# Gated projections of a four-layer triangle-multiplication kernel: low half of the weights in 64-row matmuls, pairs of units, wide units without mask

## The reference, cut to what matters

```python
xn = layer_norm(_gn(x), norm_a, norm_b)
left = (xn @ Wl + bl) * sigmoid(xn @ Wlg + blg)
right = (xn @ Wr + br) * sigmoid(xn @ Wrg + brg)
out_gate = sigmoid(xn @ Wog + bog)
out = einsum('bkjd,bkid->bijd', left, right) / n
out = layer_norm(out, on_a, on_b) * out_gate
x = x + (out @ Wo + bo)
```

## Time and profile before

| | us |
|---|---|
| median of 3 runs | 2210.91 (2204.99 to 2215.15) |
| the profiled execution | 2208.5 |
| its span in the profile | 2206.5 |
| eight `project` stages, from first matmul to last product | 562.3 |

### The profile page before, as it was taken

The page is one execution under the profiler, slowest core; times in us unless marked ns, Lnnn a source line. Parts: engine busy times, 40 slices in busy tenths (PEclk is TensorE's granted clock), DMA queues, the critical chain, the costliest instruction groups (busy, mean ns, idle before and its releaser), DMA issues. The chain is left out here.

```text
span 2206.5 us, 46371 instructions
## 1 busy us (share of the span) xinstructions
PE 1972.7 (89%) x13956; PEld 1401.8 (64%) x13956; DVE 1735.3 (79%) x2934; ACT 1691.9 (77%) x2730; POOL 624.5 (28%) x590
## 2 busy tenths in 40 slices
PE   5798979699898998989989899899998989899998
PEld 4433959455433988965633598886553369798665
DVE  6788899989588977878958897877766888687665
ACT  3588869789888857759978785776997877596676
POOL 0100828265200000026410280742871000000655
PEclk8899999999999999999999999999999999999999
DMA  9488938279788928259969973917997984663798
GB/s 396 163 263 285 280 88 229 82 286 381 243 267 264 319 77 294 88 216 398 414 211 283 272 195 120 286 52 263 407 389 226 278 293 158 222 203 124 282 357 305
DMA packets 429367, 549.52 MB, mean 249 GB/s; under 512 B 14640, under 2 KB 325936, under 8 KB 412848
## 3 DMA queue, kind: packets, MB, share of 16 engines
q1 hardware_dynamic: 427648, 538.38, 72.6%
q10 hardware_dynamic: 1584, 9.51, 1.1%
HBM read 371.67 MB, written 176.16 MB: 248 GB/s over the span
## 5 line engine op out<-in xcount | busy, mean ns | idle before, releaser
L798 PE MATMUL bank<-whigh,kept 128*128 128x128 f16 x4096 | 507.7, 228 | 62.2 <-DMA kept<-XH 21.7
L798 PEld LDWEIGHTS bank<-whigh,kept 128*128 128x128 f16 x4096 | 466.5, 125 | 69.7 <-issue 56.2
L798 PE MATMUL bank<-wlow,kept 128*128 128x128 f16 x4096 | 506.7, 227 | 0.0
L798 PEld LDWEIGHTS bank<-wlow,kept 128*128 128x128 f16 x4096 | 467.1, 125 | 0.0
L1556 POOL TENSOR_TENSOR LR<-LR 128x512 f32<-128x512 f32 x128 | 186.6, 1477 | 526.9 <-DVE LR L1602 507.4
L820 ACT ACTIVATE sigs<-bank,small 128x256 f32<-128x256 f32 x512 | 236.7, 475 | 64.4 <-PE bank L798 58.0
L1547 POOL TENSOR_TENSOR LR<-LR,sum 128x2048 f32<-128x2048 f32 x30 | 136.6, 4553 | 510.7 <-DVE LR L1365 510.7
L662 PE MATMUL bank<-LR,cen 128*128 128x512 f32 x512 | 254.6, 623 | 20.9 <-DMA LR<-XT 8.6
L820 ACT ACTIVATE squares<-bank,small 128x256 f32<-128x256 f32 x512 | 236.1, 475 | 13.3 <-PE bank L798 5.6
L669 PE MATMUL bank<-LR,kst 128*128 128x512 f32 x512 | 240.9, 593 | 5.2 <-ACT LR L690 5.2
L835 POOL TENSOR_TENSOR msgs<-sigs,mask_sb 128x256 f32<-128x256 f32 x192 | 125.9, 670 | 381.8 <-ACT sigs L820 375.3
(11 more groups left out here) (174 smaller groups left out, 3745.3 us busy)
## 6 DMA issues: line engine op xcount, KB each, us to landing
kept<-XH SPq DMA_DIRECT2D x128, 512.0 KB, 5.5
LR<-XT SPq DMA_DIRECT2D x64, 1024.0 KB, 9.4
kept<-XHA SPq DMA_DIRECT2D x128, 512.0 KB, 4.6
LR<-XT SPq DMA_DIRECT2D x112, 512.0 KB, 5.5
XT<-LR SPq DMA_DIRECT2D x56, 1024.0 KB, 8.4
LR<-XH SPq DMA_DIRECT2D x64, 512.0 KB, 6.6
LR<-XHA SPq DMA_DIRECT2D x64, 512.0 KB, 5.8
OS<-kept SPq DMA_DIRECT2D x12, 2048.0 KB, 7.6
```

The lines of the kernel that those rows point to most:

```text
L798: last = pe.matmul(bank(g)[:, j * P:(j + 1) * P], tokens, w[:, half * P:(half + 1) * P], start=part == 0, stop=part == 1)
```

## The change

- Rows: in DRAM and in the chunk buffers the channels' rows are no longer interleaved high, low, high, low, but in two blocks of 64 partitions: for side 0 high then low, for side 1 low then high (`XH` and `XHA` have four blocks in front). The rows of the projected weights follow (`K_DROP`, `K_LAST`); the output gate's 64 columns keep the old order, so `project_pe` makes six matmuls instead of three, DVE one more small operation in `fold`, and the constants have 256 more columns.
- `wlow` is multiplied only by the high rows: 64-row matmuls, on partitions 0 to 63 for side 0 and 64 to 127 for side 1, in turn. The product low x wlow is dropped.
- Order on PE: a unit q is two banks, one for each side (`bank(2q)`, `bank(2q+1)`). PE does the eight 128-row matmuls of one unit, the eight of the next, then the sixteen 64-row ones of both. It waits before a unit's 128-row matmuls until the products of the unit four before it are done.
- Layers without mask: ACT and DVE take a whole unit, 128x512, in one instruction. Masked layers keep 128x256 groups.
- `store_xh` of the layers without mask issues four DMAs of 64 partitions for a chunk instead of two of 128 (`per` is 64 for all).

```diff
@@ -115,8 +115,8 @@
             return s
 
         XT = nc.dram_tensor("XT", [NT, 8, P, COLS], F32).ap()
-        XH = nc.dram_tensor("XH", [NT, C, 2, 2, 8, 8, 256], F16).ap()
-        XHA = nc.dram_tensor("XHA", [C, 2, 2, NT, N // 2, P], F16).ap()
+        XH = nc.dram_tensor("XH", [NT, 4, C, 8, 8, 256], F16).ap()
+        XHA = nc.dram_tensor("XHA", [4, C, NT, N // 2, P], F16).ap()
         OS = nc.dram_tensor("OS", [NT, N // 16, P, 2, 256], F32).ap()
 
 
@@ -260,20 +260,21 @@
         def xh_rows(n, s, k_is_b):
 
             if k_is_b:
-                return XH[bass.ds(n // 8, 1), :, :, s, :, bass.ds(n % 8, 1), :] \
-                    .rearrange("o c w v g f -> (o c w) v (g f)")
-            return XHA[:, :, s, :, bass.ds(8 * n, 8), :].rearrange("c w t j a -> (c w) t (j a)")
+                return XH[bass.ds(n // 8, 1), 2 * s:2 * s + 2, :, :, bass.ds(n % 8, 1), :] \
+                    .rearrange("o w c v g f -> (o w c) v (g f)")
+            return XHA[2 * s:2 * s + 2, :, :, bass.ds(8 * n, 8), :].rearrange("w c t j a -> (w c) t (j a)")
 
         def store_xh(sp, n, part, buf, k_is_b, stored_):
 
             if k_is_b:
                 for s in range(2):
-                    sp.dma_start(XH[bass.ds(n // 8, 1), :, part, s, :, bass.ds(n % 8, 1), :]
+                    sp.dma_start(XH[bass.ds(n // 8, 1), 2 * s + (part ^ s), :, :, bass.ds(n % 8, 1), :]
                                  .rearrange("o c v g f -> (o c) v (g f)"), xh_cols(buf[s::2, :], k_is_b)) \
                         .then_inc(stored_.s, 16)
             else:
-                sp.dma_start(XHA[:, part, :, :, bass.ds(8 * n, 8), :].rearrange("c s t j a -> c s t (j a)"),
-                             xh_cols(buf, k_is_b)).then_inc(stored_.s, 16)
+                for s in range(2):
+                    sp.dma_start(XHA[2 * s + (part ^ s), :, :, bass.ds(8 * n, 8), :].rearrange("c t j a -> c t (j a)"),
+                                 xh_cols(buf[s::2, :], k_is_b)).then_inc(stored_.s, 16)
 
         def xh_cols(buf, k_is_b):
 
@@ -320,18 +321,21 @@
...
             def project_pe(pe):
-                pe.wait_ge(folded.s, folded.n + (3 if late else 2))
-                pe.matmul(projected_w, K(K_DROP, C), wfold, start=True, stop=False)
-                pe.matmul(projected_w, blast, w_cat, start=False, stop=False)
-                pe.matmul(projected_w, K(K_LAST, 1), prm[0:1, W_BIAS:W_BIAS + 320],
-                          start=False, stop=True).then_inc(weights.s, 1)
+                pe.wait_ge(folded.s, folded.n + (4 if late else 3))
+                for cols, drop, blast_, end in ((slice(0, 256), K_DROP, blast, K_LAST),
+                                                (slice(256, 320), K_DROP_GATE, blast_gate, K_LAST_GATE)):
+                    pe.matmul(projected_w[:, cols], K(drop, C), wfold[:, cols], start=True, stop=False)
+                    pe.matmul(projected_w[:, cols], blast_, w_cat[:, cols], start=False, stop=False)
+                    last = pe.matmul(projected_w[:, cols], K(end, 1), prm[0:1, W_BIAS:W_BIAS + 320][:, cols],
+                                     start=False, stop=True)
+                last.then_inc(weights.s, 1)
                 if late:
                     pe.matmul(centered_w, K(K_CENTER_OUT), wout_w, start=True, stop=True)
                     pe.matmul(biased_w, w_out, vec(V_OB), start=True, stop=True).then_inc(late_folded.s, 1)
...
@@ -747,14 +752,19 @@
             k_is_b, masked = layer["k_is_b"], layer["masked"]
             whigh, wlow = halves_of_w[number % 2]
             dest = LRb if layer["low"] else LR
-            gate, unscale = msg if masked else sig, unscales[number % 2]
+            unscale = unscales[number % 2]
             by_vector, by_pool = (1, 5), (0, 2, 3, 4, 6, 7)
+            each = 2 if masked else 1
+            wide_gate = [v[:, u * BANK:(u + 1) * BANK].rearrange("p (c s m) -> p c s m", s=2, m=4)
+                         for v in rings[0] for u in range(2)]
 
             def where(n, g):
 
-                if k_is_b:
-                    return g // 4, 16 * n + 4 * (g % 4)
-                return g // 2 % 2, P * (g // 4) + 8 * n + 4 * (g % 2)
+                q, s = divmod(g, 2)
+                return s, 16 * n + 4 * q
+
+            def both_sides(q):
+                return banks[q][:, :].rearrange("p (s m c) -> p c s m", s=2, m=4)
 
             @block.sync
             def _(sp):
...
-                        sp.wait_ge(projected.s, projected.n + 8 * n - 24)
+                        sp.wait_ge(projected.s, projected.n + 4 * each * n - 12 * each)
...
+                sides_last = [(s, j) for j in range(4) for s in range(2)]
+
+                def tokens(h, s, q, j, rows):
+                    x = xh_b[h][s]
+                    if k_is_b:
+                        return x.rearrange("p (b r) -> p b r", r=16)[rows, :, 4 * q + j]
+                    return x[rows, (4 * q + j) * P:(4 * q + j + 1) * P]
+
                 with pe.Fori(0, NCH // 4) as i:
                     for h in range(4):
                         pe.wait_ge(landed[h].s, landed[h].n + 32 * i + 32)
-                        for g in range(8):
-                            pe.wait_ge(products_ready.s, products_ready.n + 32 * i + 8 * h + g - 7)
-                            for j in range(4):
-                                x = xh_b[h][g // 4]
-                                if k_is_b:
-                                    tokens = x.rearrange("p (b r) -> p b r", r=16)[:, :, 4 * (g % 4) + j]
-                                else:
-                                    tokens = x[:, (4 * (g % 4) + j) * P:(4 * (g % 4) + j + 1) * P]
-                                for part, w in enumerate((whigh, wlow)):
-                                    last = pe.matmul(bank(g)[:, j * P:(j + 1) * P], tokens,
-                                                     w[:, half * P:(half + 1) * P], start=part == 0, stop=part == 1)
-                            last.then_inc(projected.s, 1)
+                        for two in range(2):
+                            for q in (2 * two, 2 * two + 1):
+                                unit = 16 * i + 4 * h + q
+                                pe.wait_ge(products_ready.s, products_ready.n + each * unit - 3 * each)
+                                for s, j in sides_last:
+                                    pe.matmul(bank(2 * q + s)[:, j * P:(j + 1) * P], tokens(h, s, q, j, slice(0, P)),
+                                              whigh[:, half * P:(half + 1) * P], start=j == 0, stop=False)
+                            for q in (2 * two, 2 * two + 1):
+                                for s, j in sides_last:
+                                    rows = slice(C * s, C * s + C)
+                                    last = pe.matmul(bank(2 * q + s)[:, j * P:(j + 1) * P], tokens(h, s, q, j, rows),
+                                                     wlow[rows, half * P:(half + 1) * P], start=False, stop=j == 3)
+                                    if j == 3 and (masked or s == 1):
...
+                else:
+                    with act.Fori(0, NCH // 4) as i:
+                        for h in range(4):
+                            for q in range(4):
+                                unit = 16 * i + 4 * h + q
+                                act.wait_ge(projected.s, projected.n + unit + 1)
+                                if half == 1 and q >= 2:
+                                    act.wait_ge(summed.s, summed.n)
+                                act.wait_ge(products_ready.s, products_ready.n + unit - 3)
+                                act.activation(wide_gate[q], both_sides(q)[:, C:, :, :],
+                                               ACT.Sigmoid, scale=unscale).then_inc(gates_ready.s, 1)
...
+                else:
+                    with dve.Fori(0, NCH // 4) as i:
+                        for h in range(4):
+                            for q in range(4):
+                                unit = 16 * i + 4 * h + q
+                                m = 8 * (4 * i + h) + 4 * (q % 2)
+                                dve.wait_ge(gates_ready.s, gates_ready.n + unit + 1)
+                                dve.scalar_tensor_tensor(dest[:, q // 2, :, :].rearrange("p c (s r) -> p c s r", s=2)
+                                                         [:, :, :, bass.ds(m, 4)],
+                                                         both_sides(q)[:, 0:C, :, :], unscale, wide_gate[q],
+                                                         ALU.mult, ALU.mult).then_inc(products_ready.s, 1)
...
@@ -925,11 +965,12 @@
             ut, vb = at(c)
             for part in range(2):
                 buf = homes.xh[c % len(homes.xh)][part]
+                blocks = slice(0, 4, 3) if part == 0 else slice(1, 3)
                 if layer["k_is_b"]:
-                    sp.dma_start(buf, XH[ut, :, part, :, vb, :, :].rearrange("c s g f -> c s (g f)")) \
```

(7 more changed lines are left out.)

97 lines of the change are left out of this document (48 added, 49 removed).

## The result

The changed kernel takes **2245.15 us**, the median of 4 runs (2239.93 to 2246.47); the kernel before, in 4 runs beside it, 2207.95 (2203.84 to 2215.15). The ratio is 1.0161, with a 95% interval of 1.0144 to 1.0177: 1.6% slower. The profiled execution has a span of 2242.7 us, against 2206.5 before, so 36.2 us are to be found.

What follows compares the result with a forecast made beforehand. PE sets the pace before; after the change, the way round of a pair of units through ACT, POOL and DVE. Masked stages 28, unmasked 3, stores 3, fold and constants 2: +36 on 2208.5, forecast 2244 us, range 2196 to 2297.

Steps and rivals of the forecast that it cites:

- The way round with mask, 4.56 us a chunk: Masked `project` stages: PE to ACT, POOL, DVE and back for a pair of units takes 4.56 us a chunk, against 4.01.
- The masked stages, +28: Four masked `project` stages: thirteen slower chunks each, a longer end, -0.5 in the first three chunks; +28 us in all.
- The overlap of 64-row matmuls: PE, both sides in turn: between 0.056 and 0.028 us each (0.063 and 0.032 with mask); the lower bound was taken.
- The switch, 0.19 and 0.15: PE changing between 128-row and 64-row matmuls loses 0.19 us one way, 0.15 back, once each for two units.
- No mask, 13 x 0 = 0: Unmasked `project` stages: a chunk stays at 3.57 us; with end and half clock +0.7 a stage, +3 us for four.
- Stores, +3: SP's queue in unmasked layers: four DMA issues instead of two delay first loads, +1.5 in each of two layers, +3 us.
- The contractions, 0: Contractions after the `project` stages: no term of their own; DMA load sizes and what `finish` reads unchanged, 0.
- The rival on the clock: `project` chunks: PE's clock falls, half of the thirteen at 0.107 us a matmul; +92 to the forecast, 2336 us; chance 0.09.
- Fold and constants, +2: Weight fold and start: three more matmul pairs, one small DVE operation, 0.13 MB more constants; +2 us (0 to 4).
- the free switches: PE in `project`: switches between row counts cost nothing with f16; chunks 4.37 and 3.38 us, total 2224 us; chance 0.12.
- No overlap: PE in `project`: 64-row matmuls don't run side by side; +86, 2294 us; chance 0.20.
- a way round that doesn't bind: `project` stages: shorter wide instructions and hand-overs leave DVE's 3.85 and PE's 3.37 as bounds; -12, 2196 us; chance 0.15.

Runs made afterwards that it cites:

- unit by unit: The changed kernel with each unit's 64-row matmuls straight behind its own 128-row ones, not after two units; 2238.42 us, 1.0136 against the kernel before.

## Why the prediction was right, and where not

The forecast was 2244 us, the result 2245.15. The sum of +36 agrees with 36.2 in the spans. The sign and the main step were right; that the sum came out to within 1 us is luck, since two errors of 15 us in it cancel.

- **The way round with mask, 4.56 us a chunk.** Measured 4.53. This is the step that decided the sign, and three runs hold it up: without the masking the waits go (3.59), with a shorter lag they go (4.19), and with slower matmuls in the same order the chunk hardly grows (4.6). 13 x 0.52 is 6.8 a stage, as forecast (+7.2). The switch in it was 0.15 instead of 0.19 (half of the 0.30 for strided tokens), so 4.52 should have come out: the hand-overs taken from the rows were right to about 0.01 in sum.
- **The masked stages, +28.** Measured +31.5. The second gives +12.1 where the others give +4.4, +6.5 and +8.6. Its thirteen chunks take 63.81 us instead of 54.03, with three chunks of 5.87, those with the table load; unit by unit, too, had them slower in this stage alone (58.2 against 54.4). The prediction took this stage for one like the other three: loads of 1.28 us, of which a PE-bound stage hid about half, lie open once the way round binds. No run takes the loads out.
- **The overlap of 64-row matmuls.** The lower bound was right: sixteen in eight slots, at either level of the clock. They took 0.028 us each without mask, not the estimated 0.036 (0.55 us less the switch, over sixteen).
- **The switch, 0.19 and 0.15.** Mis-sized: 0.10 and 0.10 without mask; with strided tokens 0.30 for both, nearly the forecast's 0.34. The rows behind it were f32 matmuls; no row of before had an f16 switch, and the rival beside it had only 0.
- **No mask, 13 x 0 = 0.** One of the two terms that failed most. Measured 3.32 a chunk, -3.4 us a stage. Putting the two measured terms in its layout, one switch of 0.10 for 0.19 (-0.09) and two ACT instructions of 0.684 for 0.739 (-0.11), gives 3.37. I had taken the length from another line of `finish`, with other operands. The other 0.05 is not accounted for. The tail was as said (2.27 us, forecast 2.41). Together -12.1 instead of +3.
- **Stores, +3.** None of it. SP does issue four instead of two, in 2.55 us:

```profile
733.52 2.55 SPq L276 DMA_DIRECT2D XHA<-LR  x4
736.11 1.30 SPq L312 DMA_DIRECT2D kept<-XHA  x2
```

  but the first three chunks and the wait in front of them take as long as before (17.03 us after and 16.75 before; 18.06 and 18.40 at the other layer; the wait 3.89 and 3.88 at both). With a DMA share above 1 in these chunks the transfers most likely set their pace, so that a later issue is hidden; no run tries that.
- **The contractions, 0.** The other term that failed, missing in the sum: +14.5. The prediction had the longer tail, +0.3 and +1.05 us, and counted it as time only. With it seven of the eight contractions start at half clock, and filling it took back 12.3 of the 14.5. The rival on the clock looked for a drop inside the chunks, where there was none in seven of the eight stages (1.00) and a small one in the second masked stage (0.95).
- **Fold and constants, +2.** The six pairs take 18.17 to 20.80, 2.6 us instead of 2.0, as said.

So the errors were -15 without mask, +3.5 with mask, -3 for stores and +14.5 for contractions.

Of the rivals, the free switches came nearest in mechanism: without mask about half the price was real, with mask nearly all of it. No overlap and, for the masked stages, a way round that doesn't bind are refuted. Without mask the chunk came out near this last rival's, 3.32 against 3.37, but by other terms: PE's own need is 3.11, and the way round still adds 0.2.

## What to carry to other kernels

Before putting like work together to save switches, lay out the lag from the last instruction of a group to the moment its buffers are free, and count how many groups still take turns: halving these made a PE that is 10% faster on its own wait for products. PE can pay again at the start of the next stage for idling longer at the end of one, through its clock; a few matmuls in the gap (here 28, 1.74 us) brought back 8 us of 37 here, and nothing where few stages started at half clock. An interruption that a stage partly hides while another engine is its bound, here a table load of 1.28 us, is paid nearly in full once it stands in the way round. And a length taken from another line's instruction is a bound, not a price: 0.739 for 0.684 us and 0.19 for 0.10 explain some 10 of the 15 us by which the stages without mask were misjudged.

## What was new of the hardware

- Two matmuls on different 64 rows, each with its own weights, start 0.003 to 0.004 us apart and share a slot of 0.056 us (0.107 at half clock); those on the same rows don't.
- PE takes a matmul on the other rows ahead of up to about four earlier ones (sixteen in 0.78 us with partners four places apart, 1.03 with eight), so with four the alternating order in the code is worth one slot of nine at most.
- A stream of 128-row matmuls and of 64-row ones on one half of the rows, without a gap, ran at a granted clock of 0.50; with the 64-row ones on both halves in turn it ran at 1.00. In the whole program PE was at half clock for 1098 us of 2629.8, against 222.5 of 2242.7. Busy time alone doesn't keep this clock up; what does was not tried further.
- A change between 128 and 64 rows with f16 cost 0.10 us each way with adjacent tokens, and 0.30 us for both with tokens 16 elements apart.
- After the same standstill PE's clock fell at one stage and not at another (2.79 us: one of four before the change; 2.11 us: three of four after it, one of four with the masked stages as before); with 0.44 to 1.28 us it fell at none of sixteen.
